# A graph network and mixture-of-experts kernel: bias by a two-row product on TensorE, gate and relu on ScalarE

## The reference, cut to what matters

```python
def _moe_forward(x, Wr, br, W1, b1, W2, b2):        # D, F, E, K = 512, 64, 8, 2
    logits = xf @ Wr + br
    probs = softmax(logits)
    vals, idx = top_k(probs, K)
    cw = (one_hot(idx, E) * vals[..., None]).sum(axis=1)
    for e in range(E):
        h = relu(xf @ W1[e] + b1[e])
        y = h @ W2[e] + b2[e]
        out = out + cw[:, e, None] * y
```

## Time and profile before

| | |
|---|---|
| median of 3 runs | 2694.34 us |
| profiled execution, its own time | 2695.04 us |
| its span, first to last instruction | 2693.4 us |
| mean granted TensorE clock | 0.992 |
| busy: TensorE, VectorE, ScalarE, POOL | 98%, 67%, 47%, 37% |
| experts' stage | about 1944 us to the end |

### The profile page before, as it was taken

How to read it: one execution, slowest core, us unless ns; L and a number is a source line. 1 busy time by engine, 2 the same in 40 slices (tenths; PEclk the granted TensorE clock), 3 DMA queues, 4 the chain that set the end, 5 groups by cost and what they waited for, 6 DMA issues and landing times.

```text
span 2693.4 us, 39731 instructions
## 1 busy us (share of the span) xinstructions
PE 2629.3 (98%) x9195; PEld 1508.0 (56%) x9195; DVE 1806.5 (67%) x5090; ACT 1270.8 (47%) x2681; POOL 992.5 (37%) x1054
## 2 busy tenths in 40 slices
PE   7999999999899999999899999999899999999999
PEld 3444445554588855555488865555455555555554
DVE  5555555554799955555599965555477777777775
ACT  2222245554488855555288855555222222222222
POOL 2222255553344445554233335555222222222221
PEclk9999999999999999999999999999999999999999
DMA  4344378886255568887245558888422222222221
GB/s 133 133 133 132 118 224 271 264 273 224 88 164 164 164 201 269 273 263 259 90 164 164 164 181 268 268 272 264 148 85 86 82 83 90 85 82 83 89 85 48
DMA packets 200943, 446.57 MB, mean 166 GB/s; under 512 B 34383, under 2 KB 34695, under 8 KB 200836
## 3 DMA queue, kind: packets, MB, share of 16 engines
q0 software_dynamic: 64928, 207.55, 26.7%
q10 hardware_dynamic: 69168, 126.12, 12.8%
q1 hardware_dynamic: 66740, 111.54, 11.8%
HBM read 238.50 MB, written 207.11 MB: 165 GB/s over the span
## 4 chain that ended last, share of the span: by engine, by line
PE 95%; DMA 2%; DVE 1%; ACT 1%; issue 1%; SPq 0%; DVEq 0%; POOL 0%; ACTq 0%; POOLq 0%
PE psY L602 11%; PE psY L582 10%; PE psH L582 10%; PE psM L713 9%; PE psY L713 8%; PE psH L713 8%; PE psT L576 6%; PE psY L616 6%; PE psY L624 5%; PE psY L633 5%; PE psS L725 4%; PE psS L726 4%; PE psM L582 2%; PE psH L602 2%; PE psS L576 1%; PE psH L809 1%
## 5 line engine op out<-in xcount | busy, mean ns | idle before, releaser
L510 POOL DMA_INDIRECT rows<-y_rows,lists x471 | 487.3, 1035 | 473.9 <-PE psS L726 313.5
L1186 DVE TENSOR_TENSOR lows<-rows,highs 128x512 fp32r<-128x512 f32 x471 | 326.1, 692 | 374.5 <-ACT highs L842 341.4
L517 POOL DMA_INDIRECT rows<-sum_rows,nodeI x237 | 296.0, 1249 | 338.7 <-DVE rows L1194 305.2
L842 ACT ACTIVATE outs<-psS 128x512 f32<-128x512 f32 x471 | 279.6, 594 | 284.9 <-PE psS L726 251.3
L842 ACT ACTIVATE highs<-rows 128x512 fp32r<-128x512 f32 x471 | 294.6, 625 | 144.1 <-ACT outs L842 98.6
L725 PE MATMUL psS<-highs,sel 128*128 128x512 f32 x471 | 348.8, 740 | 7.3 <-ACT outs L842 7.3
L491 POOL TENSOR_TENSOR st<-st,small 128x1 f32<-128x1 f32 x158 | 90.0, 570 | 663.2 <-DVE st L1086 663.2
L602 PE MATMUL psY<-wy,res 128*128 128x512 f32 x632 | 287.0, 597 | 0.8 <-ACT res L842 0.8
L582 PE MATMUL psY<-wy,xTs 128*128 128x512 f32 x632 | 285.8, 595 | 0.0
L582 PE MATMUL psH<-wz,hTs 128*128 128x512 f32 x632 | 284.2, 592 | 0.7 <-ACT hTs L842 0.7
L713 PE MATMUL psM<-wz,res 128*128 128x512 f32 x544 | 255.4, 592 | 0.0
(11 more groups left out here) (166 smaller groups left out, 4108.9 us busy)
## 6 DMA issues: line engine op xcount, KB each, us to landing
sum_rows<-outs ACTq DMA_DIRECT2D x471, 256.0 KB
y_rows<-outs SPq DMA_DIRECT2D x237, 256.0 KB
rows<-in_x POOLq DMA_DIRECT2D x78, 256.0 KB, 2.9
outs<-in_x SPq DMA_DIRECT2D x78, 256.0 KB
out_rows<-res SPq DMA_DIRECT2D x78, 256.0 KB, 2.0
rows<-y_rows,lists POOLq DMA_INDIRECT x471
rows<-sum_rows,nodeI POOLq DMA_INDIRECT x237
wy<-in_L_gnn_Wl SPq DMA_DIRECT2D x3, 1024.0 KB, 7.2
```

Of the source, the lines that this page charges most:

```text
L510: pool.indirect_dma_start(out=rows[:, t % RING, :], out_offset=None, in_=y_d, in_offset=bass.IndirectOffsetOnAxis(ap=col(srcT, t), axis=0) ...
L517: pool.indirect_dma_start(out=rows[:, s, :], out_offset=None, in_=s_d, in_offset=bass.IndirectOffsetOnAxis(ap=col(nodeI, t), axis=0), boun ...
L842: act.activation(o, i_, ACT.Copy).then_inc(signal, 1)
L1186: dve.tensor_tensor(lows[:, t % RING, :], rows[:, t % RING, :], highs[:, g, :].bitcast(F32), ALU.subtract)\
```

## The change

b1 is added on TensorE: `up` ends with one more matmul, whose stationary operand `pair` is two rows of ones at partitions 32 and 33, and whose moving operand `b1s` has the high part of b1 in one row and the low part in the other. VectorE no longer touches the hidden values. ScalarE gets `gated`: for each of eight experts one ACTIVATE, relu of scale times the 64 columns in PSUM, where scale is the row's gate, written to `outs`. SP loads b1 as two rows in place of the broadcast row, and VectorE splits it (`split_b1`) before the stage's first tile. VectorE waits for `hg_sb` of two tiles back before it overwrites the gates.

```diff
             def up(i, c):
                 t, s, n = at(i, c, 2)
                 pe.wait_ge(hg_sb[s], n)
-                product(psY[s][:, :], xTs[:, s], wy, y_ps[s])
+                product(psY[s][:, :], xTs[:, s], wy, last=False)
+                pe.matmul(psY[s][:, :], pair, b1s, start=False, stop=True).then_inc(y_ps[s], 1)
...
             pe.wait_ge(wy_in, 16 * (LAYERS + X))
+            pe.wait_ge(b1_set, 2)
             up(0, 0)
...
+            def gated(i, c):
+                t, s, n = at(i, c, 2)
+                act.wait_ge(y_ps[s], LAYERS * uses(s) + n + 1)
+                act.wait_ge(cw_set[s], n + 1)
+                act.wait_ge(hT_ps[s], n)
+                for e in range(X):
+                    g_ = act.activation(outs[:, 2 + s, e * F:(e + 1) * F], psY[s][:, e * F:(e + 1) * F], ACT.Relu,
+                                        scale=sm[:, s, CW + e:CW + e + 1])
+                g_.then_inc(hg_sb[s], 1)
...
             for i in turns(act, PAIRS - 1, True):
                 for c in (1, 2):
+                    gated(i, c - 1)
                     take_xT(i, c + 1)
                     exps(i, c)
                     take_hT(i, c - 1)
                     norm(i, c + 2)
+            gated(PAIRS - 1, 0)
             take_xT(PAIRS - 1, 2)
             exps(PAIRS - 1, 1)
             take_hT(PAIRS - 1, 0)
+            gated(PAIRS - 1, 1)
             exps(PAIRS, 0)
             take_hT(PAIRS - 1, 1)
+            gated(PAIRS, 0)
             take_hT(PAIRS, 0)
...
-                    load_row(bvec, b1.rearrange("e f -> (e f)"), bvec_in)
+                    for k in range(2):
+                        sp.dma_start(b1raw[k:k + 1, :], b1.rearrange("e f -> (e f)").unsqueeze(0)).then_inc(b1_in, 16)
                     load_w(wz, W2.rearrange("e f d -> (e f) d"), wz_in)
...
+            def split_b1():
+
+                dve.wait_ge(b1_in, 32)
+                link(copy(b1high.bitcast(F32R), b1raw))
+                link(dve.tensor_tensor(b1raw, b1raw, b1high, ALU.subtract))
+                link(dve.tensor_scalar(b1raw, b1raw, ident[two, 4 * X + 1:4 * X + 2], None, ALU.mult))
+                dve.scalar_tensor_tensor(b1s, b1high, ident[two, 4 * X:4 * X + 1], b1raw, ALU.mult, ALU.add).then_inc(b1_set, 1)
+                dve.tensor_scalar(pair, iota[two, :], 0.0, None, ALU.is_ge).then_inc(b1_set, 1)
...
                 else:
+                    split_b1()
                     dve.wait_ge(avec_in, 16)
...
+                    dve.wait_ge(hg_sb[s], n)
                     k_cw = step(dve.tensor_tensor(gate(CW), gate(LG), gate(EX), ALU.add))
-                    h = outs[:, 2 + s, :]
-                    h3 = h.rearrange("p (e f) -> p e f", e=X)
-                    dve.wait_ge(y_ps[s], LAYERS * uses(s) + n + 1)
-                    dve.wait_ge(hT_ps[s], n)
-                    k_h = step(dve.tensor_tensor(h, psY[s][:, :], bvec[:, :], ALU.add))
...
-                    after(k_h)
-                    dve.scalar_tensor_tensor(h3, h3, 0.0, gate(CW).unsqueeze(2).to_broadcast([P, X, F]),
-                                             ALU.max, ALU.mult).then_inc(hg_sb[s], 1)
...
-            AHEAD, OWN = 6, 11
+            AHEAD, OWN = 6, 10
...
-            dve.wait_ge(bvec_in, 16 * (LAYERS + 1))
```

More of the change, by code:

```diff
@@ L123, in build @@
         headT = lists[:, ET:2 * ET]
-        cwT = nc.alloc_sbuf_tensor_at("cwT", [4 * X, 2, P], F32R, offset=lists_at)
+        cwT = nc.alloc_sbuf_tensor_at("cwT", [4 * X + 2, 2, P], F32R, offset=lists_at)
         highs = nc.alloc_sbuf_tensor_at("highs", [P, 4, D], F32R, offset=hw_at)
         xTs = nc.alloc_sbuf_tensor_at("xTs", [P, 2, C, P], F32, offset=hw_at)
-        b2s = nc.alloc_sbuf_tensor_at("b2s", [4 * X, D], F32R, offset=hw_at + 8 * D)
+        b2all = nc.alloc_sbuf_tensor_at("b2s", [4 * X + 2, D], F32R, offset=hw_at + 8 * D)
+        b2s = b2all[0:4 * X, :]
         avec = nc.alloc_sbuf_tensor_at("avec", [P, D], F32, offset=hw_at + 12 * D)
@@ L158, in build @@
         smi = lists[:, 2 * P:2 * P + 8].bitcast(U32)
+        two = slice(4 * X, 4 * X + 2)
+        pair, b1s = cwT[two, 0, :], b2all[two, :]
+        b1raw, b1high = outs[two, 2, :], outs[two, 3, :]
         zeros = tmp(24, D)
@@ L185, in build @@
         b2_in = sem("b2_in")
+        b1_in = sem("b1_in")
+        b1_set = sem("b1_set")
         b2_set = sem("b2_set")
@@ L407, in _ @@
             sp.wait_ge(b2_set, 1)
-            sp.dma_start(b2_d, b2s[:, :].bitcast(F32)).then_inc(b2_st, 16)
+            sp.dma_start(b2_d, b2s.bitcast(F32)).then_inc(b2_st, 16)
             for l in range(LAYERS):
@@ L428, in _ @@
                     sp.wait_ge(b2_st, 16)
-                    sp.dma_start(b2s[:, :].bitcast(F32), b2_d).then_inc(b2_back, 16)
+                    sp.dma_start(b2s.bitcast(F32), b2_d).then_inc(b2_back, 16)
                 if l + 1 == LAYERS:
@@ L807, in down @@
                 pe.wait_ge(cw_sb[s], n + 1)
-                pe.matmul(psH[:, :], cwT[:, s, :], b2s[:, :], start=False, stop=True).then_inc(o_ps[s], 1)
+                pe.matmul(psH[:, :], cwT[0:4 * X, s, :], b2s, start=False, stop=True).then_inc(o_ps[s], 1)
             pe.wait_ge(small_in, 32)
@@ L964, in take_hT @@
                 act.wait_ge(cw_ps[s], n + 1)
-                copy(cwT[:, s, :], psS[1][0:4 * X, 0:P], cw_sb[s])
+                copy(cwT[0:4 * X, s, :], psS[1][0:4 * X, 0:P], cw_sb[s])
+            def gated(i, c):
[7 more added lines that the diff above has]
+                g_.then_inc(hg_sb[s], 1)
             all_turns(act, z_ps, LAYERS)
@@ L1070, in split_b2 @@
                 link(dve.tensor_scalar(b2raw, b2raw, is_low, None, ALU.mult))
-                dve.scalar_tensor_tensor(b2s[:, :], b2high, is_high, b2raw, ALU.mult, ALU.add).then_inc(b2_set, 1)
+                dve.scalar_tensor_tensor(b2s, b2high, is_high, b2raw, ALU.mult, ALU.add).then_inc(b2_set, 1)
+            def split_b1():
[5 more added lines that the diff above has]
+                dve.tensor_scalar(pair, iota[two, :], 0.0, None, ALU.is_ge).then_inc(b1_set, 1)
             def carry(k):
```

## The result

The changed kernel takes 2748.75 us (median of 4 runs, 2748.3 to 2750.18) against 2695.41 us (2692.85 to 2696.75) for the kernel before on the same chip: a ratio of 1.0198, 95% interval 1.0184 to 1.0212. The forecast was 2747.0 with a range of 2738 to 2768.

A forecast was written before the change was run, and what follows sets the result against it. TensorE, busy throughout the experts' stage, was taken as the bound. Bias products 47.4, start 5.0 and filling turn 0.3 sum to 52.7 on the profiled 2695.04, 2747.7; less 0.7 for the median, 2747.0 us, range 2738 to 2768.

The forecast's parts named there:

- TensorE sets the turn: Experts' loop: the 9.28 us turn is the sum of TensorE's instructions; whatever is added there is paid 79 times.
- 0.60 us for a product: TensorE, after `up`: each added bias product costs 0.60 us, priced from L809; 79 of them make 47.4 us.
- Rival B: TensorE's bias product costs 0.23 us, like a full-height F32R product; turn of 9.5, 2722 us; chance 0.08.
- The bound of 0.67: Upper bound per bias product on TensorE: 0.09 us lost both ways, 53 us in all, a time of 2753.
- The gates are covered: ScalarE's eight gates take 1.95 us and end 0.25 us before hidden_turn needs them; cost 0.
- rival A: ScalarE's gates don't overlap, take 2.66 us and make hidden_turn 0.55 late; 21 us more, 2768; chance 0.22.
- less than 0.5 before hidden_turn: Sign of being right: the gates' last end on ScalarE comes less than 0.5 us before hidden_turn.
- none of that changes length: The chain from router through VectorE, POOL and `norm` ahead of the gates keeps its length; removed operations stand behind L1086.
- Half of a lateness: If the gates come late by x, a turn costs x/2, since the next router on TensorE has gone ahead.
- 5.0 us at the start: Stage start: VectorE waits for b1 and splits it, reaching the first tile 5.0 us later; bounds 4.0 and 7.3.
- The filling turn: First turn of the stage: hidden_turn waits for the gates, up to 0.8 us once, taken as 0.3.
- Rival C: TensorE's bias product lies in its neighbours' shadow; only the start's 5 us is left, 2700 us; chance 0.04.

The follow-up runs named there:

- the full-height run: Changed kernel with the b1 product taken over all 128 array rows, padded with zeros, in place of 2 rows: 2720.65 us, ratio 1.0094.
- the split gates: Changed kernel with the same gates in 24 narrower ACTIVATEs a tile in place of 8: 2819.24 us, ratio 1.0458.
- the b2 edit alone: Kernel before with the b2 product over all 128 rows, zeros beneath the 32: 2669.24 us, ratio 0.9903.

## Why the prediction was right, point by point

**TensorE sets the turn.** Right. The turn grew by the new instruction alone, and nothing else that was moved in the stage changed it.

**0.60 us for a product.** 0.61, and its parts as read from L809: 0.09 in, 0.42 to the next start, 0.10 in `down`'s first piece. The forecast took the price from L809, which also uses only a part of the array's rows, and not from the F32R product over all 128 rows (0.23); the full-height run shows that this was the difference. Rival B is out for the change as it stands, with a turn of 9.89 and not 9.5. 47.4 us forecast, 48.2 found. The bound of 0.67, by which the way out costs as much as the way in, was not reached.

**The gates are covered.** Right in what it gives, 0, and rival A is out: TensorE never waits for the gates after the filling turn. But the cover was 1.0 and not 0.25 us, so the sign "less than 0.5 before hidden_turn" failed (1.17). The step "none of that changes length" failed: POOL's shift operation on that chain fell from 0.72 to 0.18 us, 0.54. The other 0.23 is the gates' own length, 1.72 in place of 1.95: their starts are 0.20 apart, not the 0.23 that I put between 8 and 128 columns. Rival A, at 0.22, was given too much for this reason. One of the eight lasts 0.32 us on average, they overlap, and all eight take 1.72.

**Half of a lateness.** Not needed for the result, but shown by the split gates: a wait in every second turn.

**5.0 us at the start.** 4.3: the split took 2.59 (2.54 forecast), but b1 landed 1.76 us after VectorE was free, where I had 2.4. A transfer of 2 KB was taken at the landing time of 256 KB, 2.0 us; both rows of b1 were there 1.73 us after the first issue at 1943.88. TensorE stood 11.54 us, not 12.2.

**The clock.** The sum has no term for it; my estimate was 0, with 2 us either way. It cost 1.7 us for a second fall in the profiled execution, 0 in another. **The filling turn** 0.5 in place of 0.3, and only 0.15 of it is the gates, to which the 0.3 was given; the rest is the clock's later return.

The terms that were off: 0.8 more for the products, 0.7 less at the start, 0.2 more for the filling and 1.7 for the clock, with the stage 0.6 earlier. Together 1.4 us more than forecast. That the error is so small is in part luck, since the first two cancel, though none of them alone would have led out of the range. Rival C, not slower, is out: nothing of the product lay in the shadow of its neighbours.

## What to carry to other kernels

Where one engine is full, read the price of an added instruction from the starts on either side of the nearest instruction of the same shape, and not from its busy time; the number of partitions belongs to the shape. A matmul on a few rows of the array in the midst of full ones cost 0.61 us here and the same sum padded with zeros to 128 rows 0.23, so look for such products that are already there: the b2 product held 28 us. And work taken off an engine that isn't the bound is worth what it frees for its neighbours, which was nothing here.

## What the runs showed of the hardware that was not expected

A POOL operation on 128x1 values takes 724 ns on average beside VectorE's L1384, which reads two operands from SBUF, and 183 to 188 ns where that operation is gone: in the changed kernel, in the one without the bias product, and in the two with the gates on ScalarE and b1 on VectorE. With the b2 edit alone, where VectorE keeps the operation, it stays at 722 ns. The row of the changed kernel, from 1970 to 2640 us:

```profile
L566 POOL TENSOR_TENSOR st<-st 128x1 f32<-128x1 f32 x68 | 12.5, 183 | 5.7
```

In the kernel before it starts at 2210.05, just after L1384 (2210.03), and ends when that does. L491, which runs beside L1377 with its one operand in PSUM, takes 569 ns with and without it. The profile shows it only as a longer POOL operation (724 in place of 183 ns), not as a wait, and by what mechanism it comes about is not shown.

And TensorE's clock falls not only after long stands: with 1.0 us of waiting in every second turn the granted clock fell to 0.50 for 3.4 us time and again over the whole stage, twelve times from 2000 us to TensorE's last product. No other trace here has a fall in that part of the stage.
